# Selected keys spread over the heads' blocks by 16 transfers per pair of chunks in place of two POOL products

## The reference, cut to what matters

```python
x = layernorm(x + attention(x))        # 16 heads of 8; normed q and k; tanh soft cap at 50; causal
x = layernorm(x + routed_block(x))

# routed_block: of each chunk 63 tokens are selected by a router
weights = (x @ router_w)[..., 0] + router_b[0]
topv, topi = top_k(weights, 64); thr = topv[:, -1]
sel_idx = sort(topi[:, :63]); x_sel, pos_sel, w_sel = gathered at sel_idx
m_sel = attention_mask gathered at (sel_idx, sel_idx)
hn = rmsnorm(x_sel, ln1)
q = rope(heads(hn @ wq)); kk = rope(heads(hn @ wk)); v = heads(hn @ wv)
sc = q . kk / sqrt(8) + m_sel          # per head, 63 x 63
o = softmax(sc) @ v @ wo
x1 = x_sel + o; x2 = x1 + gelu(rmsnorm(x1, ln2) @ w1) @ w2
out = zeros; out[sel_idx] = x2 * w_sel; return out + x * (weights <= thr)
```

## Time and profile before

| | us |
|---|---|
| median of 3 runs | 792.43 (791.93 to 793.32) |
| the profiled execution's own time | 795.73 |
| its span in the profile | 793.9 |
| PE busy | 650.0 (82%) |
| DVE busy | 596.5 (75%) |
| ACT busy | 553.3 (70%) |
| POOL busy | 386.2 (49%) |
| the 16 products on POOL that make `k_wide` | 30.1 busy, 1901 ns each |

### The profile page before, as it was taken

How to read it: one execution, slowest core, us unless ns; L and a number is a source line. 1 busy time by engine, 2 the same in 40 slices (tenths; PEclk the granted TensorE clock), 3 DMA queues, 4 the chain that set the end, 5 groups by cost and what they waited for, 6 DMA issues and landing times.

```text
span 793.9 us, 16532 instructions
## 1 busy us (share of the span) xinstructions
PE 650.0 (82%) x6384; PEld 373.9 (47%) x6384; DVE 596.5 (75%) x1649; ACT 553.3 (70%) x403; POOL 386.2 (49%) x399
## 2 busy tenths in 40 slices
PE   3387777889989998999989998999899979855742
PEld 2243323455546454555546454545464546344432
DVE  3651636765897889888988898788998887687656
ACT  0399887786988798879788978788798969500000
POOL 5244545536555475556646564556547653511210
PEclk9558667778989998899889988898999878965755
DMA  6303030405230323040412121030303040000001
GB/s 199 67 2 80 12 69 1 81 2 107 81 80 2 69 66 82 28 67 15 66 44 53 30 53 55 19 64 4 64 28 68 2 68 28 14 1 28 0 1 53
DMA packets 97855, 36.72 MB, mean 46 GB/s; under 512 B 69090, under 2 KB 95090, under 8 KB 97778
## 3 DMA queue, kind: packets, MB, share of 16 engines
q1 hardware_dynamic: 97778, 35.67, 20.4%
HBM read 14.69 MB, written 4.19 MB: 24 GB/s over the span
## 4 chain that ended last, share of the span: by engine, by line
PE 45%; DVE 27%; ACT 12%; issue 9%; POOL 4%; DMA 2%; SPq 1%; DVEq 0%; ACTq 0%; POOLq 0%
PE ps_y L1187 15%; PE ps_s L1170 10%; ACT pr L723 8%; ACT th L708 4%; PE ps_m L1286 3%; DVE wins L934 2%; POOL pr L619 2%; DVE qn_v L842 2%; PE ps_m L1371 1%; PE ps_a L1236 1%; PE ps_a L1218 1%; DVE v_aug L836 1%; DMA k_st<-st 1%; PE ps_m L1270 1%; PE ps_m L1194 1%
## 5 line engine op out<-in xcount | busy, mean ns | idle before, releaser
L708 ACT ACTIVATE th<-ps_s 128x1024 f32<-128x1024 f32 (+1 forms) x256 | 278.6, 1129 | 77.1 <-PE ps_s L1170 67.5
L619 POOL TENSOR_TENSOR pr<-pr,tri 128x320 f32<-128x320 f32 (+1 forms) x256 | 188.2, 757 | 192.9 <-ACT pr L723 192.8
L723 ACT ACTIVATE pr<-th 128x2304 f32<-128x2304 f32 x128 | 271.5, 2122 | 8.7 <-PE ps_y L1187 8.4
L1170 PE MATMUL ps_s<-q_st,k_st 32*64 32x512 f16 (+7 forms) x2048 | 190.8, 315 | 42.5 <-ACT th L708 34.6
L1187 PE MATMUL ps_y<-pr,v_aug 128*32 128x512 f32 (+7 forms) x2048 | 171.6, 469 | 7.8 <-POOL pr L619 7.6
L1170 PEld LDWEIGHTS ps_s<-q_st,k_st 32*64 32x64 f16 x2048 | 92.1, 114 | 168.0 <-issue 63.5
L633 POOL TENSOR_TENSOR st<-qk,st 128x1024 f16<-128x1024 f32 x32 | 76.7, 2417 | 49.5 <-DVE st L852 49.5
L1187 PEld LDWEIGHTS ps_y<-pr,v_aug 128*32 128x32 f32 x2048 | 58.3, 116 | 76.7 <-issue 47.6
L621 POOL TENSOR_TENSOR k_wide<-qkT,head_of 128x1024 f32<-128x1024 f32 x16 | 30.1, 1901 | 41.6 <-DVE qkT L1017 41.6
L694 ACT ACTIVATE sc<-hu 128x512 f32<-128x512 f32 x8 | 5.0, 630 | 64.3 <-POOL hu L621 64.3
L934 DVE SCALAR_TENSOR_TENSOR wins<-w_wide,x,later 128x512 f16<-128x512 f32 (+1 forms) x64 | 41.2, 644 | 2.6
(11 more groups left out here) (224 smaller groups left out, 1074.0 us busy)
## 6 DMA issues: line engine op xcount, KB each, us to landing
x_in<-in_L_attn_x SPq DMA_DIRECT2D x16, 256.0 KB, 3.5
x_res<-in_L_attn_x SPq DMA_DIRECT2D x16, 256.0 KB, 2.8
result<-y_out SPq DMA_DIRECT2D x16, 256.0 KB, 2.2
mask_a<-in_L_ffn_attention_mask SPq DMA_DIRECT2D x3, 1024.0 KB, 5.4
pr<-in_L_ffn_attention_mask SPq DMA_DIRECT2D x2, 1024.0 KB, 7.9
w_sb<-in_L_ffn_w SPq DMA_DIRECT2D x2, 256.0 KB
q_st<-st SPq DMA_TRANSPOSE x16, 4.5
k_st<-st SPq DMA_TRANSPOSE x16, 4.8
```

What stands on the lines that cost most here:

```text
L619: return nc.gpsimd.tensor_tensor(buf, buf, tri[:, None, :].to_broadcast([P, blocks, 64]), ALU.mult)
L708: nc.scalar.activation(th[:, gi % 2, c0:c1], ps_s[:, c0:c1], ACT.Tanh, scale=1.0 / (QK_SCALE ** 2 * DH ** 0.5 * SOFTCAP))\
L723: nc.scalar.activation(pr[:, probs_at(n):probs_at(n) + GROUP], th[:, gi % 2, :], ACT.Exp, scale=SOFTCAP).then_inc(exp_done, 1)
L1170: last = mm(ps_s[64 * s:64 * s + 64, COL[kb]:COL[kb] + S - 64 * kb], k_st[rows, k, gi // 2, 64 * kb:64 * kb + 64], q_st[rows, k, gi // 2, ...
```

## The change

`att.kw` and `head_of` go away. In their place SP issues 16 transfers per pair (`widen`), one per head: the 8 rows of that head, two chunks of 64 slots, from `qkT` to the head's block in `k_wide`, which is 8 rows with two pieces of 256 bytes in each, 4 KB. The zeros around them are written once, by a memset of the whole of `k_wide` on POOL in the setup. `widen` waits for `sel.qkT`, and for `att.S1` of the pair before. `att.S0` and `att.S1` wait until all 16 have landed. As `k_wide` must keep its zeros, `PT` moves: the first half to `hb`, the second to `RT`. Three waits are added for that on DVE: `sel.RT` waits for `att.PV` of the pair before, `sel.qkT` for `att.S1` of the pair before, `att.h` for `att.PV` of its own pair. The tables of order stay but for `att.kw`.

```diff
-    "att": ["kw0", "kw1", "hh", "hu"],
+    "att": ["hh", "hu"],
...
-    [], ["att.kw@-1"],
+    [], [],
...
-        PT = k_wide[:, 0].rearrange("p h s -> p (h s)").rearrange("p (n c) -> p n c", n=H // 2)
+        PT = [hb[:, :].rearrange("p (n c) -> p n c", n=H // 4), RT]
...
+            def widen(q):
+
+                ve["sel"].wait(sp, q, "qkT")
+                pe["att"].wait(sp, q - 1, "S1")
+                if q == 0:
+                    sp.wait_ge(k_wide_zero, 1)
+                for h in range(H):
+                    rows = slice(DH * h, DH * h + DH)
+                    sp.dma_start(k_wide[rows, :, h, :], qkT[rows, 1, :].rearrange("p (k s) -> p k s", k=2))\
+                        .then_inc(keys_wide, 16)
+
...
                 if live(p + 1, PAIRS):
                     turn(Batch(p, 2), 0)
+                if live(p - 1, PAIRS):
+                    widen(p - 1)
...
-            nc.gpsimd.memset(head_of[:, :], 1.0).then_inc(const_ready, 1)
...
             nc.gpsimd.memset(pm[:, :, :], 0.0).then_inc(zeroed, 1)
+            nc.gpsimd.memset(k_wide[:, :, :, :], 0.0).then_inc(k_wide_zero, 1)
+            pool.wait_ge(k_wide_zero, 1)
...
-            def att_kw(q, _):
-                ve["sel"].wait(pool, q, "qkT")
-                pe["att"].wait(pool, q - 1, "PV")
-                for k in range(2):
-                    pl["att"].done(mul(
-                        k_wide[:, k], qkT[:, 1, None, SLOTS * k:SLOTS * k + SLOTS].to_broadcast([P, H, SLOTS]),
-                        head_of[:, :, None].to_broadcast([P, H, SLOTS])), f"kw{k}", q)
-
...
+                [(pe["att"], lambda q: q - 1, "PV")])
...
+                [(pe["att"], lambda q: q - 1, "S1")])
...
+                pe["att"].wait(v, q, "PV")
...
             def att_scores(q, h):
-                pl["att"].wait(t_, q, "kw1")
+                t_.wait_ge(keys_wide, 16 * H * (q + 1))
...
```

More of the change, by code:

```diff
@@ L455, in build @@
         gate_ready = sem("gate_ready")
+        keys_wide = sem("keys_wide")
+        k_wide_zero = sem("k_wide_zero")
         turned = [sem(f"turned{i}") for i in range(2)]
@@ L579, in _ @@
             nc.gpsimd.iota(after_i, pattern=[[-P, NT]], base=S - 1, channel_multiplier=-1).then_inc(const_ready, 1)
-            pool.wait_ge(const_ready, 9)
+            pool.wait_ge(const_ready, 8)
             nc.gpsimd.affine_select(out=ident[:, :], in_=ident[:, :], compare_op=ALU.not_equal, fill=1.0, base=0,
@@ L586, in _ @@
                                     pattern=[[1, S]], channel_multiplier=-1).then_inc(const_ready, 1)
-            nc.gpsimd.affine_select(out=head_of[:, :], in_=head_of[:, :], compare_op=ALU.is_ge, fill=0.0, base=0,
-                                    pattern=[[-DH, H]], channel_multiplier=1).then_inc(const_ready, 1)
             nc.gpsimd.affine_select(out=half_of[:, :, :], in_=half_of[:, :, :], compare_op=ALU.is_ge, fill=0.0, base=0,
@@ L592, in _ @@
             nc.gpsimd.tensor_copy(after16, after_i).then_inc(const_ready, 1)
-            pool.wait_ge(const_ready, 16)
-            nc.gpsimd.affine_select(out=head_of[:, :], in_=head_of[:, :], compare_op=ALU.is_ge, fill=0.0, base=DH - 1,
-                                    pattern=[[DH, H]], channel_multiplier=-1).then_inc(const_ready, 1)
+            pool.wait_ge(const_ready, 14)
             nc.gpsimd.affine_select(out=half_of[:, :, :], in_=half_of[:, :, :], compare_op=ALU.is_ge, fill=0.0,
@@ L664, in att_hu @@
                 pl["att"].done(mul(hu[:, :], hq[:, :], hb[:, :]), "hu", q)
-            table = {"prep.sq": prep_sq, "prep.lo": prep_lo, "route.xw": route_xw, "sel.zb": sel_zb, "att.kw": att_kw,
+            table = {"prep.sq": prep_sq, "prep.lo": prep_lo, "route.xw": route_xw, "sel.zb": sel_zb,
                      "att.hh": att_hh, "att.hu": att_hu}
@@ L739, in _ @@
             v.wait_ge(attn_weights_in, 16 * 7)
-            v.wait_ge(const_ready, 19)
+            v.wait_ge(const_ready, 16)
             v.wait_ge(setup_pe, 1)
@@ L990, in _ @@
             sel_RT = copy_step("sel", "RT", lambda: nc.vector.tensor_copy(
-                RT[:, :, :], at("sel.RT")[:, :].rearrange("p (c s) -> p c s", c=NT)))
+                RT[:, :, :], at("sel.RT")[:, :].rearrange("p (c s) -> p c s", c=NT)),
+                [(pe["att"], lambda q: q - 1, "PV")])
             sel_hnT = copy_step("sel", "hnT", lambda: nc.vector.tensor_scalar(
@@ L1017, in _ @@
             sel_qkT = copy_step("sel", "qkT", lambda: nc.vector.tensor_copy(
-                qkT[:, :, :], at("sel.qkT")[:, 0:2 * P].rearrange("p (s c) -> p s c", s=2)))
+                qkT[:, :, :], at("sel.qkT")[:, 0:2 * P].rearrange("p (s c) -> p s c", s=2)),
+                [(pe["att"], lambda q: q - 1, "S1")])
             def att_scores(q, h):
@@ L1043, in att_PT @@
                 chain(ve["att"], q)(lambda: nc.vector.tensor_copy(
-                    PT[:, 4 * h:4 * h + 4, :], at(f"att.P{h}")[:, :].rearrange("p (n s) -> p n s", n=4)), f"PT{h}")
+                    PT[h][:, :, :], at(f"att.P{h}")[:, :].rearrange("p (n s) -> p n s", n=4)), f"PT{h}")
             def att_PV(q, _):
@@ L1146, in _ @@
             tr = nc.tensor.transpose
-            t_.wait_ge(const_ready, 19)
+            t_.wait_ge(const_ready, 16)
             t_.wait_ge(attn_weights_in, 16 * 7)
@@ L1347, in att_PV @@
                 for n in range(H // 2):
-                    last = mm(at("att.PV")[:, 32 * n:32 * n + 32], PT[:, n, :], vv[:, n, :, :].rearrange("p k c -> p (k c)"),
+                    last = mm(at("att.PV")[:, 32 * n:32 * n + 32], PT[n // 4][:, n % 4, :], vv[:, n, :, :].rearrange("p k c -> p (k c)"),
                               start=True, stop=True)
```

1 line of the change is left out of this document (removed).

## The result

The changed kernel takes **892.09 us** (median of 4 runs, 889.56 to 893.84) beside 792.18 of the kernel before on the same chip: ratio 1.127, with an interval of 1.122 to 1.132. That is slower, as forecast, but by 100 us and not by 42, and outside the range of 811 to 858.

What follows compares the result with a forecast made beforehand. PE (45% of the span) and DVE (27%) were taken to hand the bound to each other. 31.5 us of late `att.S0` plus 10.5 us of clock made 42, added to the median 792.43: 834 us, range 811 to 858.

Steps and rivals of the forecast that it cites:

- slack: From the end of the `qkT` copy to `att.S0`: time the transfers have before holding up PE, 34.9 us over eight pairs.
- the same formula: Loss at `att.S0` over eight pairs: 8 x 8.3 - 34.9 = 31.5 us by which PE and DVE come late.
- The landing term: Time from the last SP issue to its landing: 1.8 us, taken from the smallest rows.
- the pitch of 0.43 us: Time between SP issues in a bunch of 16, a mean of four rows; bounds 0.37 and 0.66 us.
- the prediction's own sign of being wrong: Wrong if `att.S0` doesn't wait, pairs grow less than the gap, or an issue takes under 0.2 or over 0.6 us.
- the upper end of the bound: Dearest issue on SP, 0.66 us from `w_o`: keys spread 12.2 us after the copy, a loss of 62.7 us.
- Rival (b): An issue on SP as dear as that of `w_o`: 866 us, to 876 with the longer fall; chance 0.11.
- the clock's fall: PE at half clock behind the `att.S0` gap: 2.1 us in pairs two to six, 10.5 us; bounds 0 and 21.
- the edits at nothing: Setup memset of `k_wide`, copies into `hb` and `RT`, and three new DVE waits: no cost.
- (c): PE's gap at `att.S0` is made good before the pair is over: 792 to 794 us; chance 0.05.
- (d): SP issues small transfers in under 0.14 us, so the gap vanishes: 792 us, 785 at the least; chance 0.03.
- (a): The cheapest issue on SP and no fall of the clock: 19 to 24 us, 811 to 817; chance 0.20.

Runs made afterwards that it cites:

- p1_probe: Kernel before plus eight bunches of extra SP transfers at its end: an issue took 0.59 to 0.69 us within SBUF, 0.295 for 8 rows from HBM.
- p2_probe: Kernel before plus nine bunches of other transfer forms at SP's end: 0.30 us an issue for 8 rows with HBM on one side, 0.589 for one row within SBUF.
- f1_flat: Changed kernel with `k_wide` laid out so that each transfer is 8 rows in one piece: 877.5 us, ratio 1.107, an issue 0.624 us.
- d2_dummy9: Changed kernel with nine unused products on PE ahead of its wait for the transfers: 862.38 us, ratio 1.089.
- w1_warm: Kernel before with unused products on PE ahead of two of its own gaps, at `att.h2T` and `fin.wo`: 796.49 us, ratio 1.007.
- h1_half: Changed kernel with only the 8 transfers of the even heads, the odd heads' keys left out: 839.41 us, ratio 1.059.
- d1_dummy: Changed kernel with seven unused products on PE ahead of its wait for the transfers: 870.67 us, ratio 1.099.

## Why the prediction was right on the direction and wrong on the size

**Right: where the loss arises.** The slack was measured as the time from the copy to `att.S0`, 34.9 us over eight pairs. With the third pair's 12.84 us in place of 8.3 the same formula gives 8 x 12.84 - 34.9 = 67.8 us, and with all eight as they were (104.6 us) 69.7; PE waited for 67.7. Both engines of the chain came late, as said: DVE's `att.sc0` waited for 77.2 us where it waited for 1.0 in the kernel before. The landing term of 1.8 us measured 1.84, and SP did begin 0.03 us after the copy.

**Wrong, the larger part: the pitch of 0.43 us.** It measured 0.73: 15 x 0.30 x 8 = 36 us too little. By the prediction's own sign of being wrong, an issue of over 0.6 us, it was. The step that failed is the choice of the nearest row. Of the earlier trace rows I took those that were like the new transfers in bytes and number of pieces. All of them load from HBM, and this is what made them cheap: the same 8 rows of 512 bytes take 0.295 us from HBM and 0.624 within SBUF (p1_probe), and even one row within SBUF takes 0.59 (p2_probe). Bytes, rows and pieces, by which I had chosen, hardly count between two places in SBUF. The prediction did say that the trace has no transfer between two places in SBUF; the upper end of the bound, 0.66 from `w_o`, stood for that, and even it was too low for the pitch. That it came near is luck: `w_o` is loaded from HBM with two pieces in a row, a form that takes 0.67 in p1_probe, while the new transfers are dear in one piece too (f1_flat). Rival (b), 866 to 876, was the nearest of the cases, and had been given 0.11. A slip beside it: the range's end of 858 goes with a pitch of 0.55 us only if the clock's fall takes its upper bound of 21 us; with the 10.5 of the sum it allows 0.63.

The rule of the Trainium skill weighed there ("DMA: Bandwidth & Descriptors", section "Issuing engines are not separate DMA queues": the time to initiate a DMA "is usually small relative to the DMA itself") doesn't fit here, and less so than the prediction thought: one issue's 0.73 us is 40% of the landing of 1.84 us and not a fifth to a quarter, and the 16 took 11.66 us, over six times one landing.

**Wrong, the smaller part: the clock.** I had put 2.1 us on one fall, for five pairs: 10.5 us. It was 3.7 us in all eight: 30 us by d2_dummy9, above the upper bound of 21. Two factors of the term failed. The length: 3.4 us of half clock, taken from rows near 425 us, where 9.4 followed in the third pair and 7.5 on the mean of the eight. And the count: the first pair and the last two were to be spared, but the products of `att.S0` ran at half clock in each. The price of one us of half clock was not too low: 2.1/3.4 = 0.62 forecast, 30/60 = 0.5 measured, and 0.5 is all that half clock can take from an engine that works without a pause. It was read from the difference of two pairs, 84.0 against 81.9, as if nothing but the clock differed in them.

**Right: the edits at nothing.** The move of `PT` and the three waits: ratio 1.002, not told from zero. POOL's freed time brought 2 us at `pv`, of the 7.6 that were the most. The load of `x_in` and the transposing transfers that SP now issues later show no cost, by what is left over and not by a run of their own: the gap and the clock, 67.7 + 29.7 = 97.4 us, leave 2.5 of the 99.9 for everything else, about the spread of the runs.

**The rivals.** (c), the gap made good within the pair: refuted by d2_dummy9, where `att.S0` came 70.6 us late and the loss was 70.6 us. (d), that SP hands such transfers out far faster: refuted by every bunch of p1_probe, none under 0.29 us. (a) fell with the pitch.

Not tried: spreading the issues over a second engine's queue, and going through HBM (one store, then 16 loads). An estimate for the latter, from a pitch of 2.66/8 = 0.33 us (p2_probe's bunch of 8 flat loads), 2.4 us for the store (the median landing of the four times larger stores of `result` in the profile after) and 1.84 for the last landing: 2.4 + 15 x 0.33 + 1.84 = 9.2 us from the copy, still over the 4 us of slack.

## What to carry to other kernels

Price a bunch of transfers by a row that has the same kind of memory on both sides, before looking at bytes or pieces; if the trace has no such row, the forecast should start from the dearest one and not from the one that looks alike. An issuing engine's list is serial: here sixteen small transfers were sixteen issues and one landing, and the last one decides. Here a gap of some 8 us on the busy PE cost its length and a fall of the clock on top, in every pair. Price such a fall at half of all the half clock that follows, in every repeat where that engine sets the pace; elsewhere it can be nearly free, as at the first place of w1_warm.

## What the runs showed that I had not expected

- An issue on SP takes 0.30 us for 8 rows with HBM on one side, 0.43 for 128 rows from HBM, and 0.59 to 0.69 between two places in SBUF, down to a single row of 512 bytes (p1_probe, p2_probe). Two pieces per row cost 0.67 from HBM, but 0.298 towards it.
- A wait of 2.36 us went with half clock for 6.8 us (h1_half), one of 8.2 us was followed by half clock for 9.4 us of dense work; a wait of 0.28 us, with products running ahead of it, was not (d2_dummy9). With waits of about 2 us it went either way: 6.8 us of half clock behind 1.97 us, none behind 2.01 (d1_dummy).
- A higher granted clock can be worth nothing: from 0.82 to 0.857 over the whole run the time went from 791.79 to 796.49 (w1_warm). Some 3 to 7 us of half clock less in the middle of a pair brought the next steps 0.2 to 0.3 us forward in four of the pairs.
